# Cross-channel attention on one core: eleven of sixteen batches turned by VectorE instead of eight, with three group slots, seven output buffers and later stores

## The reference

```
rgb, geo = x.T, ctx.T                     # per batch, (1024, 128)
xca(q, k, v): attn = softmax(q^T k * 16**-0.5);  out = v attn      # per head, 16 x 16
res_p2r = xca(rgb wq_rgb^T, geo wk_point^T, geo wv_point^T) proj_p2r^T
res_r2p = xca(geo wq_point^T, rgb wk_rgb^T, rgb wv_rgb^T) proj_r2p^T
out = (rgb + res_p2r)^T + (geo + res_r2p)^T
```

## Time and profile before

| | |
|---|---|
| median of three runs | 129.18 us (129.02 to 129.22) |
| profiled execution, its time | 129.13 us |
| profiled execution, its span | 127.1 us |
| busy: PE, ACT, POOL, DVE | 120.8, 86.4, 77.3, 71.4 us |
| DMA moved | 34.25 MB, mean 270 GB/s |

### The profile page before, as it was taken

One profiled execution on the slowest core, in us unless ns is written; L12 is line 12 of the kernel. 1 busy time (PEld: TensorE's weight loads), 2 busy tenths in 40 slices (PEclk: granted clock), 3 DMA queues, 4 the chain that ended last, 5 costly groups with the idle time before them and its releaser, 6 DMA issues.

```text
span 127.1 us, 2678 instructions
## 1 busy us (share of the span) xinstructions
PE 120.8 (95%) x858; PEld 110.0 (87%) x858; DVE 71.4 (56%) x210; ACT 86.4 (68%) x195; POOL 77.3 (61%) x41
## 2 busy tenths in 40 slices
PE   6979999999999999999999999999999998997990
PEld 6859998899898989898989989999989897985880
DVE  0035364637878625969653787862596965546210
ACT  4133967875959595878787595959587868588351
POOL 5000779685495958195958559595819595937700
PEclk9999999999999999999999999999999999999999
DMA  3999999999999999999999999999999750003435
GB/s 102 362 398 409 419 285 252 230 289 256 296 243 251 246 328 370 328 271 281 313 274 339 380 328 282 278 280 300 329 418 419 317 233 1 0 23 147 168 142 191
DMA packets 16493, 34.25 MB, mean 270 GB/s; under 512 B 1376, under 2 KB 9952, under 8 KB 16480
## 3 DMA queue, kind: packets, MB, share of 16 engines
q1 hardware_dynamic: 11840, 29.36, 72.9%
q10 hardware_dynamic: 4640, 4.72, 14.4%
HBM read 25.69 MB, written 8.39 MB: 268 GB/s over the span
## 4 chain that ended last, share of the span: by engine, by line
PE 84%; DMA 5%; ACT 3%; issue 2%; DVE 1%; SPq 1%; ACTq 1%
PE out_ps L312 32%; PE gram_bank L291 21%; PE sy_bank L342 6%; DMA g_raw<-in_ctx_dram 5%; PE gt_ps L270 5%; PE xt_ps L270 4%; PE t_bank L355 3%; PE sy_bank L366 3%; PE sy_bank L365 3%; PE t_bank L356 3%; ACT expd L454 2%; PE uv_bank L333 1%; PE uv_bank L335 1%; PE uv_bank L334 1%; DVE probs L568 1%
## 5 line engine op out<-in xcount | busy, mean ns | idle before, releaser
L205 POOL TENSOR_TENSOR x_lo<-x_raw,x_hi 128x1024 fp32r<-128x1024 f32 x16 | 38.0, 2378 | 39.0 <-ACT x_hi L425 39.0
L208 POOL TENSOR_TENSOR g_lo<-g_raw,g_hi 128x1024 fp32r<-128x1024 f32 x16 | 38.0, 2373 | 2.5 <-ACT g_hi L425 2.5
L291 PE MATMUL gram_bank<-gt,xt 128*128 128x128 f32 x256 | 33.8, 275 | 0.0
L291 PEld LDWEIGHTS gram_bank<-gt,xt 128*128 128x128 f32 x256 | 31.2, 192 | 0.0
L541 DVE COPY gt<-gt_ps 128x512 f32<-128x512 f32 x16 | 11.0, 687 | 18.9 <-PE gt_ps L270 18.9
L432 ACT COPY out_sb<-out_ps 128x512 f32<-128x512 f32 x31 | 18.0, 581 | 5.2 <-PE out_ps L312 3.9
L454 ACT ACTIVATE expd<-scores,min_neg 128x128 f32<-128x128 f32 x32 | 12.6, 396 | 8.6 <-DVE min_neg L551 8.6
L425 ACT CAST g_hi<-g_raw 128x1024 fp32r<-128x1024 f32 x16 | 16.9, 1055 | 0.0
L425 ACT CAST x_hi<-x_raw 128x1024 fp32r<-128x1024 f32 x16 | 16.6, 1037 | 0.0
L438 ACT COPY xt<-xt_ps 128x512 f32<-128x512 f32 x16 | 9.4, 586 | 9.1 <-PE xt_ps L270 9.1
L312 PE MATMUL out_ps<-x_hi,t_hi 128*128 128x512 f32 x31 | 13.6, 440 | 0.0
(11 more groups left out here) (80 smaller groups left out, 211.5 us busy)
## 6 DMA issues: line engine op xcount, KB each, us to landing
x_raw<-in_x_dram SPq DMA_DIRECT2D x15, 512.0 KB, 15.8
g_raw<-in_ctx_dram SPq DMA_DIRECT2D x15, 512.0 KB, 16.2
out_dram<-out_sb SPq DMA_DIRECT2D x15, 512.0 KB, 15.1
xz<-in_x_dram SPq DMA_DIRECT2D x8, 256.0 KB, 12.4
gz<-in_ctx_dram SPq DMA_DIRECT2D x8, 256.0 KB, 16.0
xz<-in_x_dram ACTq DMA_DIRECT2D x8, 256.0 KB, 11.8
gz<-in_ctx_dram ACTq DMA_DIRECT2D x8, 256.0 KB, 13.9
g_raw<-in_ctx_dram ACTq DMA_DIRECT2D x2, 256.0 KB, 4.6
```

The lines of the kernel that those rows point to most:

```text
L205: nc.gpsimd.tensor_tensor(x_lo[:, slot, :], x_raw[:, raw_slot, :], x_hi[:, slot, :].bitcast(F32), ALU.subtract).then_inc(x_lo_ready, 1)
L208: nc.gpsimd.tensor_tensor(g_lo[:, slot, :], g_raw[:, raw_slot, :], g_hi[:, slot, :].bitcast(F32), ALU.subtract).then_inc(g_lo_ready, 1)
L291: last = nc.tensor.matmul(gram_ps, xt[:, b % 2, cols], gt[:, b % 2, cols], start=(t == 0), stop=(t == TILES - 1))
```

## The change

Batches 5 to 15 are turned by VectorE, in six groups, the last of one batch: (5, 6), (7, 8), (9, 10), (11, 12), (13, 14), (15). Batches 7, 10 and 13 are new among them. There are three group slots instead of two, seven output buffers instead of five, and SyncE issues the store of batch b in its step b + 8 instead of b + 5. In a step in which a gz copy and an xz copy are both issued, gz now goes first.

```diff
-OUT_SLOTS = 5
-PAIRS = 2
+OUT_SLOTS = 7
+STORE_LAG = 8
+PAIRS = 3
...
-VECTOR_PAIRS = ((5, 6), (8, 9), (11, 12), (14, 15))
+VECTOR_GROUPS = ((5, 6), (7, 8), (9, 10), (11, 12), (13, 14), (15,))
...
-            first = VECTOR_PAIRS[pair][0]
+            first, count = VECTOR_GROUPS[pair][0], len(VECTOR_GROUPS[pair])
             for q in quads:
-                into = dst[q * QUAD:(q + 1) * QUAD, pair % PAIRS, :, :]
+                into = dst[q * QUAD:(q + 1) * QUAD, pair % PAIRS, 0:count, :]
...
-            eng.wait_ge(xt_turned, 4 * pair + 4)
-            eng.wait_ge(gt_ready, 2 * VECTOR_PAIRS[pair][1] + 2)
+            last = VECTOR_GROUPS[pair][-1]
+            eng.wait_ge(xt_turned, 2 * on_vector.index(last) + 2)
+            eng.wait_ge(gt_ready, 2 * last + 2)
...
-        issued_in = {2 + 2 * pair if pair < PAIRS else VECTOR_PAIRS[pair - PAIRS][1] + 1: pair
-                     for pair in range(len(VECTOR_PAIRS))}
+        issued_in = {2 + 2 * pair if pair < PAIRS else VECTOR_GROUPS[pair - PAIRS][-1] + 1: pair
+                     for pair in range(len(VECTOR_GROUPS))}
...
-            for i in range(2, B + 4):
+            for i in range(2, B):
...
+                if g_pair is not None:
+                    load_turned(sp, g_turn, gz, gz_loaded, g_pair, (0, 1))
                 if x_pair is not None:
                     if x_pair >= PAIRS:
                         pair_turned(sp, x_pair - PAIRS)
                     load_turned(sp, x_turn, xz, xz_loaded, x_pair, (0, 1))
-                if g_pair is not None:
-                    load_turned(sp, g_turn, gz, gz_loaded, g_pair, (0, 1))
-                if i >= 5:
-                    store(i - 5)
+                if i >= STORE_LAG:
+                    store(i - STORE_LAG)
+            for b in range(B - STORE_LAG, B - 1):
+                store(b)
```

More of the change, by code:

```diff
@@ L45, in bass_cross_channel_attention @@
     QUADS = P // QUAD
-    on_vector = [b for pair in VECTOR_PAIRS for b in pair]
+    on_vector = [b for group in VECTOR_GROUPS for b in group]
     on_tensor = [b for b in range(B) if b not in on_vector]
@@ L153, in load_turned @@
         def load_turned(eng, src, dst, loaded, pair, quads):
-            first = VECTOR_PAIRS[pair][0]
+            first, count = VECTOR_GROUPS[pair][0], len(VECTOR_GROUPS[pair])
             for q in quads:
-                into = dst[q * QUAD:(q + 1) * QUAD, pair % PAIRS, :, :]
+                into = dst[q * QUAD:(q + 1) * QUAD, pair % PAIRS, 0:count, :]
                 eng.dma_start(into.rearrange("p e (a m) -> p (e a) m", a=QUADS),
-                              src[q][:, QUADS * first:QUADS * (first + 2), :]).then_inc(loaded[pair % PAIRS], 16)
+                              src[q][:, QUADS * first:QUADS * (first + count), :]).then_inc(loaded[pair % PAIRS], 16)
         def pair_turned(eng, pair):
-            eng.wait_ge(xt_turned, 4 * pair + 4)
-            eng.wait_ge(gt_ready, 2 * VECTOR_PAIRS[pair][1] + 2)
+            last = VECTOR_GROUPS[pair][-1]
+            eng.wait_ge(xt_turned, 2 * on_vector.index(last) + 2)
+            eng.wait_ge(gt_ready, 2 * last + 2)
         def x_turned_half(eng, b, half):
@@ L477, in _ @@
                     split_hi(s, x_raw, x_loaded, x_hi, x_hi_ready)
+                if g_pair is not None:
+                    load_turned(act, g_turn, gz, gz_loaded, g_pair, (2,))
                 if x_pair is not None:
@@ L481, in _ @@
                     load_turned(act, x_turn, xz, xz_loaded, x_pair, (2,))
-                if g_pair is not None:
-                    load_turned(act, g_turn, gz, gz_loaded, g_pair, (2,))
                 if l >= 0:
@@ L493, in _ @@
                     split_hi(s, g_raw, g_loaded, g_hi, g_hi_ready)
+                if g_pair is not None:
+                    load_turned(act, g_turn, gz, gz_loaded, g_pair, (3,))
                 if x_pair is not None:
                     load_turned(act, x_turn, xz, xz_loaded, x_pair, (3,))
-                if g_pair is not None:
-                    load_turned(act, g_turn, gz, gz_loaded, g_pair, (3,))
                 if i in on_tensor:
@@ L526, in turn_half @@
             def turn_half(b, half, src, loaded, dst, turned):
-                n = on_vector.index(b)
-                pair, at = n // 2, n % 2
+                pair = [b in group for group in VECTOR_GROUPS].index(True)
+                at = VECTOR_GROUPS[pair].index(b)
                 dve.wait_ge(loaded[pair % PAIRS], 64 * (pair // PAIRS) + 64)
```

## The result

The changed kernel takes 133.81 us in the median of four executions (131.60 to 135.09), the kernel before 129.20. The ratio is 1.024 (95% interval 1.015 to 1.033). Run again on another chip it took 133.3 to 137.3 us, median 135.23, beside 129.26 of the kernel before; the ratio there is 1.035 (1.029 to 1.042). It is slower. It is also unsteady: executions of before lie within some tenths of each other (129.02 to 129.22 here), those after within 3.5 us. Ratios are made of the executions within 1.5% of a kernel's fastest, medians of all of them.

What follows compares the result with a forecast made beforehand. Two bounds side by side: TensorE's work, and DMA work arriving just in time. 129.13 us less 5.27 of transposes plus 10.4 of VectorE waiting for gz made 134.2 us, range 129.4 to 137.0.

Steps and rivals of the forecast that it cites:

- 1.26 us for a turned piece: DMA queues: price of each added 262 KB turned piece, the middle between 1.18 and 1.34 us.
- 106.0: Landing of batch 15's gz, the last gz copy, in us; 12.6 later than 93.4, and wanted at 95.6.
- the same division: Last gz landing: delay is 12 added turned pieces at 1.26 us less two store pieces at 1.25 us.
- 10.4 us forecast: VectorE's summed waits on gz, at batch 15 and earlier turns, with TensorE waiting behind it: 10.4 us.
- Growing from batch 7 and longest at 13 or 15: Expected sign: VectorE's gz waits, 10 us in sum, grow from batch 7 and are longest at 13 or 15.
- this is part of the 10.4, not on top: the bytes decide the end: Groups (7, 8), (9, 10): gz notice two steps, not three; batch 7's gz 4.0 us late, counted within 10.4.
- 123.9: Whole kernel: time in us if 48 transposes leave TensorE and all copies stay hidden; rival "all hidden", chance 0.02.
- The third group slot moves issues earlier, but a full queue does not move bytes sooner: Turned copies: a third slot lets them be issued earlier, but with full queues their bytes move no sooner.
- With steps of 8 to 9 us this is hidden: Evacuations wait for the store seven batches back, issued three steps ahead and landing within 20 us: no cost.
- The two store pieces that I counted as room gained: Store lag: stores 0 to 3 instead of 0 to 5 ahead of the last gz, two 524 KB pieces fewer.
- a fall of TensorE's granted clock: TensorE: clock case, chance 0.11; the range leaves out its top, 0.04.
- Side by side: Rival: turned copies overlapping on two queues, 0.78 us a piece, 128.6 us; below 0.83 the change wins; chance 0.09.

Runs made afterwards that it cites:

- run 2: Changed kernel with every gz copy issued one step earlier, in its xz copy's step: 126.96 to 135.80 us, median 135.03.
- run 7: Changed kernel with gz issued a step earlier and stores at lag 5 (seven buffers kept): 128.12 to 129.87 us, median 128.73, ratio 0.995.
- Runs 3 and 5: Changed kernel with the former eight batches and groups, all else kept (3): median 132.63 us; besides, five output buffers and store lag 5 (5): median 131.12.
- run 4: Changed kernel with stores at lag 5 instead of 8, still seven output buffers: 127.03 to 135.54 us, median 133.03.
- the pieces alone: Only copies, no attention computed: turned pieces and plain loads in seven phases, varying queues and partition halves; 293 GB/s halves apart, 226 mixed, 412 plain.

## Why the prediction came out as it did

**The bound.** The prediction took the full DMA queues for a second bound beside TensorE. That much held: the change took TensorE's 48 transposes away, and the time rose. The engine side was right to the tenth: steps without a wait take 6.28 us.

**The copies' price.** I took 1.26 us for a turned piece, from 1.18 and 1.34. The last gz copy, issued at 89.6, landed 15.2 us later:

```profile
L159 SPq DMA_DIRECT2D gz<-in_ctx_dram x2: 442/1902/3362, 89.1 to 89.6; - x2
...
DMA to landing us min/median/max: 12.9/14.0/15.2
```

That is 104.8 us, where I had 106.0, so the piece cost (104.8 - 93.4 + 2.5) / 12 = 1.16 us by the same division. Alone in one half of the partitions it costs 1.27, 0.89 at best, and about 1.4 beside plain loads. But the landing isn't set by the bytes alone, as the division has it: in run 2's profiled execution the last piece landed at 92.9. Ahead of it were the plain loads up to batch 12 and stores 0 to 2, five pieces of 524 KB fewer than in the kernel before, and the same division would give (92.9 - 93.4 + 6.25) / 12 = 0.48 us.

**Where the wait falls.** The sum was near, 10.4 us forecast and 11.25 found in the execution profiled, but neither its place nor what it is made of. "Growing from batch 7 and longest at 13 or 15" was wrong: batch 15's gz landed 2.2 us before it was wanted at 106.99, and the largest wait stood at batch 9. The step that failed is "this is part of the 10.4, not on top: the bytes decide the end". The largest wait came of short notice: ScalarE issued batch 9's last gz piece at 46.89, two steps ahead, and it took 18.5 us, not 15.2:

```profile
46.89 0.32 ACTq L159 DMA_DIRECT2D gz<-in_ctx_dram  x1
```

With 15.2 us it would still have been 3 us late. Of the 11.25 us, the steps of batches 7 and 9 hold 8.4 us, and those of batches 12 and 13, with the late stores, 2.6. Batch 13's gz was late with three steps of notice, since SyncE came to issue its last piece only at 77.1 and it took 17.4 us:

```profile
L159 SPq DMA_DIRECT2D gz<-in_ctx_dram x2: 2294/2772/3249, 73.8 to 77.1; - x2
...
DMA to landing us min/median/max: 10.5/14.0/17.4
```

So it is luck that the number came out: the landing that I summed never held anything up, and other waits, which I had counted inside it or at nothing, added up to nearly the same.

Run 2 and run 7 show the rest: in their profiled executions, with the notice given, the waits on gz are none and 0.9 us. What remains in run 7, about 5 us against 123.9, goes with waits for plain loads of 7.1 us; which property of the full queues makes these late stays open.

**The third slot.** "The third group slot moves issues earlier, but a full queue does not move bytes sooner" put its cost at nothing. Runs 3 and 5 show 1.6 to 3.4 us in the median, with not one copy added.

**The stores.** "With steps of 8 to 9 us this is hidden" was wrong. Two evacuations waited for stores, 4.9 us, with one on the critical chain; steps between the waits are 6.28 us, not 8 to 9, and the third store, that of batch 2, took 16.4 us from its issue at 79.42. The two store pieces that I counted as room gained brought nothing that run 4 could show.

**The clock.** The forecast gives 0.11 to a fall of TensorE's granted clock, and its range leaves out that case's top. Both were my estimate: the only run it could rest on, that of the kernel before, doesn't show the term; its granted clock is 1.00 in every window of the earlier trace rows. In its place the changed kernel showed some 6 us at half clock (0.50 from 65 to 71 us) in and behind one wait in mid-run, on top of the late copies. Its step is 1.1 us longer than the wait (7.76 less 6.61). That is a lower bound, since 0.6 us of batch 7's wait cost no time.

**Side by side.** The threshold I gave, 0.83 us a piece, wasn't reached even by the best arrangement alone, 0.89. In the pieces alone both queues in one half moved 212 GB/s and one queue 206; the two queues in different halves moved 293; whole rows moved 412.

**What I missed.** That the time would spread. The kernel before has 1.2 us of room at its last gz copy, and its 39 executions beside these runs took 128.98 to 131.23 us, all but two of them under 130.5; run 2's six, with the same copies as the changed kernel, took 126.96 to 135.80. The profiles of the changed kernel and of run 2 move 273 and 311 GB/s for almost the same work. No kernel was profiled in both a low and a high time, so whether the rate differs between executions of one kernel, and why they spread, isn't settled.

## What to carry to other kernels

A DMA share of 1 beside falling GB/s is a warning even when no engine waits (the kernel before: 1.02 at 419 GB/s, 1.06 at 297, and 1.2 us of room at its last gz copy). It gives no fixed rate: here the share was 1.07 or 1.08 at 273 and at 311 GB/s. Before work is moved from an engine to copies, price the added pieces in queue time, with the rate of their own packet size, and compare the landing of the last one with when it is wanted. Then check the notice of each copy, step by step: a copy that took 15 us in a full queue and gets two steps of 6.3 us is late whatever the sum of bytes says. And ask who else stands in that queue: in run 7 the waits went from gz to plain loads when gz was issued earlier.

## What the hardware showed that I had not expected

- Two queues that write to different halves of the partitions reached 293 GB/s in 1 KB packets; with their halves mixed, 226; both in one half, 212; one queue alone 206 to 232; whole 4 KB rows 412. Four plain loads beside eight pieces ran at 259, no faster than one after the other.
- In full queues gz pieces of 262 KB took 15.2 and 16.3 us from issue to landing in the kernel before and 12.5, 17.4 and 18.5 us in the changed one, and one kernel's executions differ by up to 9 us (126.96 to 135.80 in run 2).
- TensorE's granted clock fell to 0.50 during a stand of 5.8 us (0.69 from 64 to 65 us, 0.50 from 65 to 71) and was at 1.00 again from 72 us on.
